# Five instruction lists of a fused attention and expert kernel written in a new order

## The reference, cut to what matters

```python
h = layernorm(x)
q, k, v = h @ Wq, h @ Wk, h @ Wv            # 16 heads of 64
a = softmax(causal(q @ k.T / 8))            # 512 x 512 a head
y = layernorm(h + heads(a @ v) @ Wo) * gamma + beta
x = x + y
z = layernorm(x)
c = top-8-of-32 softmax weights of z @ gate_w.T
x = x + sum over 32 experts of c[e] * ((up_e(z) * silu(gate_e(z))) @ down_e.T)
```

## Time and profile before

| what | us |
|---|---|
| median of three runs | 1803.82 |
| the profiled execution | 1805.14 |
| its span, first to last instruction | 1803.4 |
| TensorE busy in it | 1716.6 (95%) |
| VectorE, GpSimd, ScalarE busy | 1469.4, 1314.8, 1311.8 |
| mean granted TensorE clock | 0.991 |

### The profile page before, as it was taken

How to read it: one execution, slowest core, us unless ns; L and a number is a source line. 1 busy time by engine, 2 the same in 40 slices (tenths; PEclk the granted TensorE clock), 3 DMA queues, 4 the chain that set the end, 5 groups by cost and what they waited for, 6 DMA issues and landing times. The chain is left out here.

```text
span 1803.4 us, 47581 instructions
## 1 busy us (share of the span) xinstructions
PE 1716.6 (95%) x16713; PEld 971.0 (54%) x16713; DVE 1469.4 (81%) x4477; ACT 1311.8 (73%) x2138; POOL 1314.8 (73%) x1433
## 2 busy tenths in 40 slices
PE   5898999999999999999999999999999999999978
PEld 1455555555555555555555555555555555555543
DVE  8798878888787888878888788887878888787657
ACT  3888677776877778677786877778677786867852
POOL 2577786877777777776877777777776877777870
PEclk8999999999999999999999999999999999999999
DMA  7352535435254343534435254343544425253313
GB/s 214 82 103 63 140 89 129 104 79 146 56 143 111 97 108 81 141 88 123 110 81 142 58 143 107 98 111 76 138 96 121 111 76 140 65 132 77 97 54 101
DMA packets 180512, 190.77 MB, mean 106 GB/s; under 512 B 22450, under 2 KB 146098, under 8 KB 180018
## 3 DMA queue, kind: packets, MB, share of 16 engines
q1 hardware_dynamic: 180276, 187.73, 41.4%
HBM read 81.22 MB, written 5.24 MB: 48 GB/s over the span
## 5 line engine op out<-in xcount | busy, mean ns | idle before, releaser
L1398 POOL TENSOR_TENSOR p_lo<-p,p_hi 128x1280 f16<-128x1280 f32 x256 | 670.8, 2621 | 166.9 <-ACT p_hi L729 163.3
L791 ACT ACTIVATE p<-bank_s,back 128x512 f32<-128x512 f32 (+1 forms) x768 | 455.1, 613 | 150.7 <-POOL p_lo L1398 88.8
L1040 DVE CUSTOM_DVE_ANT_0 max_junk<-bank_r,mask 128x512 f16<-128x512 f32 (+2 forms) x968 | 429.1, 485 | 64.8 <-PE bank_r L346 60.0
L346 PE MATMUL bank_s<-score_ops 128*128 128x512 f16 (+3 forms) x2048 | 393.3, 300 | 8.4 <-ACT p L791 6.7
L729 ACT ACTIVATE p_hi<-p 128x1280 f16<-128x1280 f32 x256 | 324.8, 1269 | 47.2 <-PE bank_v L346 35.3
L1425 POOL TENSOR_TENSOR expert_room<-expert_room 128x512 f32<-128x512 f32 x240 | 304.5, 1275 | 57.0 <-DVE expert_room L1138 32.3
L346 PEld LDWEIGHTS bank_s<-score_ops 128*128 128x128 f16 x2048 | 174.9, 98 | 179.4 <-ACT p L791 43.8
L346 PE MATMUL bank_v<-v_hi,p_hi 128*128 128x65 f16 x2490 | 252.2, 194 | 15.7 <-DVE o L1053 10.4
L346 PEld LDWEIGHTS bank_v<-v_hi,p_hi 128*128 128x128 f16 x2490 | 227.9, 98 | 54.2 <-DVE o L1053 22.6
L346 PE MATMUL bank_x<-expert_room,wd 128*128 128x512 f32 x480 | 251.9, 613 | 0.0
L346 PE MATMUL bank_v<-v_lo,p_hi 128*128 128x64 f16 x2490 | 251.8, 193 | 0.0
(11 more groups left out here) (204 smaller groups left out, 3126.2 us busy)
## 6 DMA issues: line engine op xcount, KB each, us to landing
score_ops<-nat SPq DMA_DIRECT2D x768, 128.0 KB, 2.5
expert_room<-comb_rows SPq DMA_DIRECT2D x480, 128.0 KB, 3.0
xt<-in_x SPq DMA_DIRECT2D x16, 256.0 KB, 3.5
xb<-in_x SPq DMA_DIRECT2D x16, 256.0 KB, 3.5
out_y<-expert_room SPq DMA_DIRECT2D x16, 256.0 KB, 2.3
score_ops<-comb_rows SPq DMA_DIRECT2D x32, 128.0 KB, 3.1
expert_room<-in_gate_up SPq DMA_DIRECT2D x1, 2048.0 KB, 10.8
score_ops<-rowmaxT SPq DMA_DIRECT2D x128, 4.0 KB
```

Source lines behind the costliest of these rows:

```text
L346: return pe.matmul(dst, lhsT, rhs, start=start, stop=stop, skip_group_check=shared)
L791: act.activation(p32[:, h % P_SLOTS, at:at + cols], bank[score_bank(h, u)][:, 0:cols], ACT.Exp, scale=back[:, SC_SCORE:SC_SCORE + 1]).then ...
L1040: done = dve.tensor_tensor_reduce(max_junk[:, k % 2, at:at + cols], bank[b][:, at:at + cols], mask[:, S - cols:S], 1.0, NEG, ALU.add, ALU. ...
L1398: pool.tensor_tensor(p_lo[:, slot, :], p32[:, slot, :], p_hi[:, slot, :], ALU.subtract).then_inc(p_lo_done, 1)
```

## The change

The lists of all five engines are replaced. Each engine has the same calls with the same arguments as before (511 on SyncE, 2900 on TensorE, 1993 on ScalarE, 2584 on VectorE, 1152 on GpSimd); 88 of TensorE's calls, all of images 0 to 2, 14 and 15, use another bank than before. No helper changes. No instruction is added or taken away. In the loop the banks stay as they were. The rows are read in the changed kernel one or two line numbers lower (L790 for L791).

Two lines of the loop's lists as a sample:

```diff
@@ TensorE, the loop
...
+                turn_maxima(n, 3, V); scores(n, 4, 0); scores(n, 4, 1); values(n, 5, R0); scores(n, 4, 2); turn_heads(n, 0, V)
+                values(n, 6, R1); times_v(n, 2, V); turn_h2(n - 1); scores(n, 5, 0); times_v(n, 3, V); logit_product(n - 1)
...
@@ GpSimd, the loop
...
-                mask_far(n, 5); mask_near(n, 5); mask_near(n, 6); p_low(n, 5); mask_far(n, 6); p_low(n, 6)
...
```

More of the change, by code:

```diff
@@ L543, in _ @@
[L543 to L547, removed]
@@ new lines, in _ @@
+            times_v(1, 1, V); scores(1, 3, 2); values(1, 5, R0); turn_maxima(1, 3, V); turn_heads(1, 0, V); scores(1, 4, 0)
+            scores(1, 4, 1); values(1, 6, R1); values(1, 7, R0); times_v(1, 2, V); scores(1, 4, 2); scores(1, 5, 0)
+            turn_h2(0); times_v(1, 3, V); scores(1, 5, 1); scores(1, 5, 2); turn_heads(1, 1, V); logit_product(0)
+            times_wo(1, 0, V); scores(1, 6, 0); turn_h(2, V); scores(1, 6, 1); scores(1, 6, 2); project(2, 0, R1)
+            project(2, 1, R0); gate_product(0, 0, G); times_v(1, 4, V); scores(1, 7, 0); max_scores(2, 0, 0, R1, R0)
@@ new lines, in _ @@
+            o_high(13, 7, V); exps(14, 2, 0); input_apply(15); exps(14, 2, 1); p_high(14, 1); exps(14, 2, 2); copy_out(12)
+            p_high(14, 2); exps(14, 3, 0); residual_apply(13); exps(14, 3, 1); v_high(14, 4, R1); exps(14, 3, 2)
+            copy_maxima(14, 3, V); exps(14, 4, 0); exps(14, 4, 1); o_high(14, 0, V); p_high(14, 3); v_high(14, 5, R0)
+            second_apply(13); v_high(14, 6, R1); h2_high(13); exps(14, 4, 2); exps(14, 5, 0); p_high(14, 4); o_high(14, 1, V)
+            v_high(14, 7, R0); gate_tanh(13, 0, G); exps(14, 5, 1); exps(14, 5, 2); route(13); exps(14, 6, 0); exps(14, 6, 1)
@@ new lines, in _ @@
+            qk_low(1, 14, R1); divide(0, 14, V); qk_low(1, 15, R0); denominators(0, 15, V); divide(0, 15, V)
+            row_maximum(1, 7, 0, 0, R1); row_maximum(1, 7, 0, 1, R0); o_low(0, 7, V); row_maximum(1, 7, 1, 0, R1)
+            row_maximum(1, 7, 1, 1, R0); add_heads(0, 3, V); residual_stats(0); row_maximum(1, 7, 2, 0, R1)
+            denominators(1, 0, V); row_maximum(1, 7, 2, 1, R0); divide(1, 0, V); rest(6); denominators(1, 1, V)
+            divide(1, 1, V); v_low(1, 4, R1); add_input(0); second_stats(0); v_low(1, 5, R0); o_low(1, 0, V)
@@ new lines, in _ @@
+            denominators(1, 2, V); rest(7); divide(1, 2, V); input_stats(3); denominators(1, 3, V); divide(1, 3, V)
+            v_low(1, 6, R1); h2_low(0); rest(8); o_low(1, 1, V); take_logits(0); choose(0); add_heads(1, 0, V); mark_chosen(0)
+            h_low(2, V); v_low(1, 7, R0); weigh(0); qk_low(2, 0, R1); qk_low(2, 1, R0); denominators(1, 4, V)
+            gate_times_tanh(0, 0, G); row_maximum(2, 0, 0, 0, R1); row_maximum(2, 0, 0, 1, R0); divide(1, 4, V)
+            gate_times_tanh(0, 1, G); row_maximum(2, 0, 1, 0, R1); row_maximum(2, 0, 1, 1, R0); denominators(1, 5, V)
```

1106 lines of the change are left out of this document (544 added, 562 removed).

## The result

The changed kernel takes 1823.49 us (median of four runs, 1822.43 to 1825.21), the kernel before 1804.53 beside it: a ratio of 1.0105, with an interval of 1.0088 to 1.0123. The prediction, 1799.0 with a range of 1789 to 1812, was on the wrong side of no change, and outside its range.

A forecast was written before the change was run, and what follows sets the result against it. TensorE, busy 95% of the span, was taken to bound the kernel. 12 x (-0.7 + 0.3) = -4.8 us, with start and end at 0, gave a median of 1799.0 us, range 1789 to 1812.

The forecast's parts named there:

- Start and end: 0.: First two and last two images: VectorE's work is the same, so no change, give or take 3 us.
- a sign of being wrong: The prediction is wrong if the difference comes from the first 150 us or the last 130.
- Step 1: Loop, `times_v` of head 1: 0.85 us wait filled by two calls, lost to a later `exps` of head 3; net 0.
- Step 2: Loop, ScalarE: `second_apply` ahead of an `exps`, `copy_weights` ahead of the waiting `gate_tanh`; 0.33 + 0.38 = 0.7 us won a pass.
- The second half of the term: Loop, ScalarE: `copy_weights` fills the gap before `gate_tanh`, winning 0.38 us a pass.
- Step 3: Middle of the pass: earlier `input_stats` and `max_scores` make TensorE wait for `row_maximum`; +0.3 us a pass, bounds 0 and 0.75.
- The rival "slower": Loop: `residual_inverse` 1.1 us later holds head 3's `exps` and part 2 of its scores; +8.4 us, 1812; chance 0.22.

The follow-up runs named there:

- step 1 alone: Kernel before, with `values` 4 and part 1 of head 3's scores ahead of `times_v`, `residual_apply` and `v_high` ahead of head 3's first `exps`: 1811.51 us.
- Its larger part alone: Kernel before, with `input_stats` of the image after the next moved directly behind the row maxima of pair 2 on VectorE: 1810.81 us.
- the two runs whose first image had one low place fewer: Changed kernel with `place_qk(n, 7)` ahead of `keep_weights`, 1817.35 us; changed kernel with head 3's first `exps` ahead of `residual_apply`, 1823.76 us.
- the run in which that `rest` took 1.28: Changed kernel with three VectorE calls of the start moved, `scale_experts` earlier and `rest(4)` and `rest(5)` later: 1819.4 us.

## Why the prediction was wrong, point by point

**"Start and end: 0."** This step failed most: the start costs 11.2 us of the 18.4, shown by the run with the old order there. (A difference from the first 150 us, here 7.2, was named as a sign of being wrong.) I argued that VectorE's work is the same; it is, but not its time. The largest named part, 6.5 us of VectorE time, stands behind GpSimd's `p_low`; taking 6.0 of them away gave back 4.1 us, TensorE's clock included. The rows of before had the sign of it (a `rest` of 1.96 beside one of 1.28), and I never looked at single durations there. The rest of the 11.2 us is located (about 2 us more in the first image, 4 in the second) but its waits were not taken apart one by one.

**Step 1, "filled, and given back. Net 0".** The mechanism was right: the `divide` wait went and one for the `exps` of head 3 came. Its size was off: 1.44 us for 1.04 alone (+0.4 a pass), and 1.81 in the changed kernel. The step that failed is the start of `residual_apply`. The `exps` at 911.3 is 909.29 + 2.0, so I let `residual_apply` take the place of the `exps`, at 909.29. But it writes bank x, which `add_experts` empties only at 909.70 (start 908.95, 0.75), 0.4 us later, and I named no wait for it. The run with step 1 alone shows it (0.34 us), and its +0.4 a pass. In the changed kernel it is 0.67, with `turn_out` one call later in TensorE's list as well. The run that put the `exps` first showed that this wait alone is not the loss.

**Step 2, "-0.7 a pass".** `second_apply` came 0.32 us sooner, as worked out (0.33), but the 0.7 was a sum of local gains without the call that pays: part 0 of head 5's scores, which waits for the `exps` put behind. Alone it is +0.6 a pass, with `turn_h2` moved too -0.2. The second half of the term, 0.38 for `copy_weights`, gave TensorE nothing. In the changed kernel TensorE's waits in this stretch, 2.4 us in the sum before, are 1.4 (0.95 of it a new one of `times_v` of head 2 for an `o_low`): about -0.95 there. That is the whole new order of the stretch, in which other calls moved too, and is not shown to be step 2's.

**Step 3, "+0.3".** Its larger part alone is +0.5, inside the bounds of 0 and 0.75, but that is luck: the wait is another than I named (`o_low`, not a row maximum). In the changed kernel no such wait is seen, so it is 0 there.

**What was missing: SyncE's list.** Six DMAs ahead of `spread_weights` cost 0.59 us a pass, shown by the run that moved them. The prediction read no SyncE row, and priced none of its moves.

The loop: +0.77 - 0.95 + 0 + 0.59 = +0.41, of 0.57 measured; the other 0.16 a pass is spread thin. The terms are waits read from the trace. Only that of SyncE's list is shown to be a loss by an edit of the changed kernel, and it is as large as the loop's whole difference; the others come to about 0 together. The rival "slower" had the sign and not the cause: `residual_inverse` is not late but 0.57 us sooner (0.18 for 0.75 behind `turn_out`).

## What to carry to other kernels

In lists that are written out for several engines, a call pulled ahead of its neighbours sends its time to whatever waits for those neighbours; find that call in the other engine's list before counting a gain. Look at single durations, not only at waits: an instruction that takes 3.2 us in one place and 1.3 in another, like `rest` here, waits inside its own busy time. And the DMA queue is a list like the others: count its issues between a store and the load that needs it.

## What the hardware showed that I had not expected

- VectorE and GpSimd held each other up for whole instructions: 2.58 us for 0.17 on a `tensor_scalar` of 128x2, 3.23 for 1.28 on a `rest`, 1.39 for 0.41 on a select.
- Six DMA issues of 128 KB each took SyncE 837.60 - 833.43 = 4.17 us, 0.7 each, and moved a dependent load by 3 us.
- From 138 to 145 us the granted clock was 0.76 in the changed kernel, behind a wait of 2.26 us at a `max_scores` (VectorE was in a `rest` of 3.16), and 1.00 in the run in which that `rest` took 1.28. In that run it was 0.86 from 160 to 172 us instead, behind waits of 0.81 and 1.58 us, beside a `rest` that had not been moved and took 3.14. At the level of 1.2 GHz for 2 x 0.24 of 7 us, 0.76 is at most 1.7 us of TensorE work lost; the two runs whose first image had one low place fewer took 0.7 to 0.8 us less for it.
